# Attention on one Trainium2 core: two shifts of 128 bytes in the on-chip buffers

## The reference

```python
q = concat([q_C, rope(c_Q @ W_QR.T)]);  k = concat([k_C, rope(xn @ W_KR.T)])
weights = softmax(where(causal, clip(q @ k.T, -80, 80), -inf) / sqrt(192))
s = (weights @ v).reshape(B, S, H * D_H) @ W_O.T
g = silu(xn @ weight + lora(xn, router))
return x + s * g
```

## The kernel before

| buffers | begins at, before | remainder by 256 | after the change |
|---|---|---|---|
| cos, sin, qr_h/l, wo_first, rows_h0/l0, scale0 | 16,512 and on | 128 | 0 |
| absorb_h/l, cq_h/l, merged_h | 43,136 and on | 128 | 0 |
| causal | 77,952 | 128 | 0 |
| ones (128 bytes) | 78,976 | 128 | 128 |
| x_all and all of prepare's own (turn_h/l at 0, xt_h/l and b_h/l at 128) | 79,104 and on | as before | as before |
| key_slot 0 to 2, value_slot 0 and 1 | 79,104 and on | 0 | 0 |
| set 1: q_h1, q_l1, rot_hh1, rot_l01; rows_h1/l1 | 87,296 and on | 0 | 0 |
| prob, prob_h, prob_l, total1 | 120,064 to 152,832 | 0 | 0 |
| total0, rows0 | 178,048 | 128 | 0 |
| set 0: rot_l00, rot_hh0, q_l0, q_h0; merged_l | 186,240 and on | 128 | 0 |
| sums, head_rows | 219,008 and on | 128 | 0 |

## Time and profile before

### The profile page before, as it was taken

The page is one execution under the profiler, slowest core; times in us unless marked ns, Lnnn a source line. Parts: engine busy times, 40 slices in busy tenths (PEclk is TensorE's granted clock), DMA queues, the critical chain, the costliest instruction groups (busy, mean ns, idle before and its releaser), DMA issues.

```text
span 1417.7 us, 27675 instructions
## 1 busy us (share of the span) xinstructions
PE 1381.3 (97%) x9810; PEld 1156.7 (82%) x9810; DVE 1144.5 (81%) x1339; ACT 781.9 (55%) x861; POOL 125.7 (9%) x175
## 2 busy tenths in 40 slices
PE   7999689999999999999999999999999999999998
PEld 6888568778788888888888889888899688878887
DVE  7666378898898898989889898898788888967664
ACT  4232357666666666666666666666656656533221
POOL 0000111201101101010010100111100011012221
PEclk9999899999999999999999999999999999999999
DMA  7332664545435333334242432444412233166552
GB/s 291 118 100 79 193 199 150 173 138 150 122 96 149 107 108 85 120 87 126 63 122 85 104 110 63 118 153 140 134 56 61 69 109 115 49 197 173 174 159 89
DMA packets 110769, 174.91 MB, mean 123 GB/s; under 512 B 9608, under 2 KB 65160, under 8 KB 108168
## 3 DMA queue, kind: packets, MB, share of 16 engines
q1 hardware_dynamic: 93880, 108.99, 24.6%
q0 software_dynamic: 16016, 63.80, 15.4%
q10 hardware_dynamic: 832, 1.57, 0.5%
HBM read 125.83 MB, written 48.50 MB: 123 GB/s over the span
## 4 chain that ended last, share of the span: by engine, by line
PE 72%; DVE 9%; ACT 3%; DMA 2%; issue 2%; POOL 0%; SPq 0%; DVEq 0%; ACTq 0%; POOLq 0%
PE score_ps L1244 29%; PE out_ps L1266 19%; PE score_ps L1363 3%; PE score_ps L1365 3%; PE score_ps L1364 3%; DVE prob_l L1560 3%; ACT prob_h L1423 2%; DVE prob L1547 1%; DVE prod L1519 1%; PE out_ps L1285 1%; PE out_ps L1289 1%; PE out_ps L1286 1%; DVE total L1555 1%; PE score_ps L1214 1%; PE score_ps L1215 1%
## 5 line engine op out<-in xcount | busy, mean ns | idle before, releaser
L1423 ACT CAST prob_h<-prob 128x1024 fp32r<-128x1024 f32 (+1 forms) x288 | 289.6, 1006 | 237.3 <-DVE prob L1542 189.6
L1560 DVE TENSOR_TENSOR prob_l<-prob,prob_h 128x1024 fp32r<-128x1024 f32 (+1 forms) x288 | 336.0, 1167 | 39.6 <-ACT prob_h L1423 38.2
L1244 PE MATMUL score_ps<-q_h,key_slot 64*128 64x512 f32 x1792 | 365.8, 390 | 0.0
L1417 ACT ACTIVATE prob<-score_ps 128x1024 f32<-128x1024 f32 (+1 forms) x288 | 281.9, 979 | 145.8 <-PE score_ps L1244 96.5
L1266 PE MATMUL out_ps<-prob_h,value_slot 64*128 64x512 f32 (+1 forms) x1792 | 351.9, 378 | 0.7
L1555 DVE TENSOR_TENSOR total<-total,prob 128x1024 f32<-128x1024 f32 (+1 forms) x256 | 294.9, 1152 | 0.0
L1542 DVE TENSOR_SCALAR prob<-prob 128x1024 f32<-128x1024 f32 x224 | 155.1, 692 | 70.4 <-ACT prob L1417 70.1
L1266 PEld LDWEIGHTS out_ps<-prob_h,value_slot 64*128 64x128 f32 x1792 | 180.8, 184 | 35.5 <-DVE prob_l L1560 6.8
L1244 PEld LDWEIGHTS score_ps<-q_h,key_slot 64*128 64x128 f32 x1792 | 180.8, 184 | 28.1 <-issue 5.1
L1244 PE MATMUL score_ps<-rot_hh,key_slot 64*128 64x512 f32 x896 | 181.8, 388 | 0.0
L1244 PE MATMUL score_ps<-q_l,key_slot 64*128 64x512 f32 x896 | 181.6, 387 | 0.0
(11 more groups left out here) (210 smaller groups left out, 2005.2 us busy)
## 6 DMA issues: line engine op xcount, KB each, us to landing
key_slot<-keys SPq DMA_DIRECT2D x144, 256.0 KB, 2.6
value_slot<-values SPq DMA_DIRECT2D x144, 128.0 KB, 2.3
rot_hh<-turned POOLq DMA_DIRECT2D x30, 512.0 KB, 6.3
heads_rows<-head_rows POOLq DMA_DIRECT2D x15, 1024.0 KB, 9.7
turned<-rot_hl POOLq DMA_DIRECT2D x14, 1024.0 KB, 5.2
rows<-heads_rows SPq DMA_DIRECT2D x28, 512.0 KB, 5.7
rot_l<-turned POOLq DMA_DIRECT2D x30, 256.0 KB, 7.6
x_in<-in_x SPq DMA_DIRECT2D x16, 256.0 KB, 2.7
```

The costliest lines, as they stand in the source:

```text
L1244: mm = pe.matmul(score_ps[:, half, c * 512:(c + 1) * 512], keys_of[ROWS[r], :], moving[par][ROWS[r], half * HW + c * 512:half * HW + (c + ...
L1417: nc.scalar.activation(prob[half][:, 0:width], score_ps[:, half, 0:width], ACT.Exp, scale=QK_SCALE).then_inc(exp_done, 1)
L1423: nc.scalar.copy(prob_h[half][:, 0:width], prob[half][:, 0:width]).then_inc(high_done, 1)
L1560: nc.vector.tensor_tensor(p_l, p, p_h, ALU.subtract).then_inc(split, 1)
```

## The change

The unused `edge` on the right grows from 24 to 56 words of float32 (96 to 224 bytes), so all of `Top` moves down by 128 bytes. `ones` (128 bytes) is allocated ahead of the cosines instead of behind `causal`, so the buffers of `Persistent` other than `ones` move up by 128 bytes, and what lies behind it stays. No instruction, wait, transfer or size of an operand changes.

```diff
 WO_FIRST = 13
-EDGE = 24
+EDGE = 56
...
+        self.ones = sb("ones", [P, 32], F32)
         ((self.cos, self.sin, self.qr_h, self.qr_l), (self.wo_first,),
...
         self.causal = sb("causal", [P, CT], F32)
-        self.ones = sb("ones", [P, 32], F32)
```

## The result

The changed kernel takes 1410.43 us (median of 5 runs, 1409.48 to 1411.62) against 1418.6 for the kernel before (5 runs, 1416.91 to 1419.74). The ratio of the mean times is 0.9945, with a 95% interval from 0.9930 to 0.9959: 7.8 us less, and 8.2 by the medians, where 7.2 were forecast. With five runs the median of the kernel before is 1418.6, where the three runs known at the forecast gave 1417.05. The profiled execution took 1410.43 us, its span is 1408.9.

What follows compares the result with a forecast made beforehand. TensorE, busy 97% of the span, was taken to bound the kernel. Attention's 5.35 us plus projection's 1.87 made 7.2 us, taking the median from 1417.05 to 1409.8 us, with a range of 1406.0 to 1413.3.

Steps and rivals of the forecast that it cites:

- The third witness: Prepare: turn_h and turn_l at 0 against b_h and b_l at 128 take 233 ns a step, slow like odd tiles.
- (a): Attention: right-hand buffers go to 0 and agree with the keys, so even units match odd ones; 5.35 us gained.
- (b): Projection: left persistent buffers go to 0, odd tiles fall from 11.17 to 10.90; seven tiles gain 1.87 us.
- Tile 1's gain is given back: Projection: tile 1 brings nothing, as TensorE waits 0.8 us for VectorE's rows_l after tile 2 and that chain doesn't shorten.
- (c) to (e): Attention's VectorE work, 6.28 us a FULL pair, fits TensorE's 6.80; cq, absorb, qr, other buffers and short stretches gain nothing.
- (e): Short stretches after the latent run at 232 ns though 0 against 0; gain between 0 and 1.9 us, taken as 0.
- Nothing moves: Rival: the units' difference comes from place in SBUF or of the code, not the remainder; 1417.0 us, chance 0.08.
- Half of it: Rival: only projection gains, 1415.2 us, chance 0.05, or only attention gains, 1411.7 us, chance 0.05.
- Slower: Rival: the regular pace needs 128, so even tiles and 256-column steps lose and attention gains nothing; 1420.8 us, chance 0.03.
- More of it: Rival: attention's short stretches after the latent speed up too, 1.9 us more; 1407.9 us, chance 0.09.
- The rule in bold: TensorE is slow where weights and moving operand have different remainders by 256 bytes, 232.0 against 226.7 ns a step in attention.

Runs made afterwards that it cites:

- e7_prepare: Changed kernel with prepare's split weights as narrow and wide tensors, so wide rows, xt, b_h, b_l, turn_h, turn_l lie at 128; 1410.56 us, ratio 0.9941 to the kernel before.
- e8_again: The changed kernel run once more, nothing altered, as a yardstick; 1410.6 us, ratio 0.9943 to the kernel before.
- e3_all_128: Kernel before plus a 128-byte pad ahead of the key slots, putting all of attention and projection at remainder 128; 1411.84 us, ratio 0.9946.
- e1_edge: Kernel before with only the edge grown from 24 to 56 words, left persistent buffers staying at 128; 1413.47 us, ratio 0.9966.
- e2_ones: Kernel before with only ones moved in front, right-hand buffers staying where they were; 1418.83 us, ratio 1.0003.
- e9_order: Changed kernel with gaps: merged_l, rows_l0 and rows_h1 at 128, merged_h, rows_h0 and rows_l1 at 0; one execution, 1414.02 us.
- e4_keys_128: Changed kernel with the key and value slots alone at 128, the rest at 0; 1425.31 us, ratio 1.0048 to the kernel before.

## Why the prediction was right

**The basis.** The forecast took one set of operands as the state before and the other as the state after, and the trace of the changed kernel shows just that: 226.7 ns a step in unit 10 and couples that are equal to 0.02 us. The third witness, the products in prepare, was the check that it is a matter of two operands; e7_prepare brought those to one remainder, and they reached 227 ns.

**How near the number is, is partly luck.** The forecast of 1409.8 lies 0.6 us below the measured median because two misses offset each other: it started from 1417.05, 1.5 us below the later median of before, and its gain of 7.2 is 1.0 us short of the 8.2 by the medians (0.6 by the ratio). The gain is made up of the parts that follow.

**(a), attention, 5.35 us.** Measured from the start of unit 0 to that of unit 15: 1108.64 - 161.78 = 946.86 before, 1103.12 - 162.00 = 941.12 after, 5.74 less. Units 6, 8, 10 and 12 gave 0.48, 0.77, 1.08 and 1.32. Units 0 to 5 together gave 0.17, where 0.23 was put for unit 4; so small a term can't be tested, for unit 4 alone took 45.59 us in the changed kernel and 46.36 in e7_prepare with the same remainders. The mis-sized term is unit 14, put at 1.54 by carrying the series on. By stretch, before:

```profile
995.18:1108.64 113.46, 113.20 (x930) 107.45 (x928) 96.52 (x97) 70.86 (x72) 4.70 (x7) 1.00 0.28 81
```

and after:

```profile
991.55:1103.12 111.57, 111.30 (x931) 96.00 (x929) 96.40 (x97) 70.91 (x72) 4.20 (x7) 1.00 0.28 82
```

The difference is 1.89 us. Unit 14 makes no rotated queries for a next couple (`has_second` is false), which leaves VectorE less to do in its first pairs; by the starts in the trace its third FULL pair already ran at TensorE's own pace (6.93 us, and 6.80 after), while unit 12's took 7.20 and 7.14. So more of its pairs run at TensorE's own pace than two more pairs would add, and each of them gains. That the lighter load of VectorE is the cause is argued from the code. Carrying on a series of units was sound only while they had the same work.

**(b), projection, 1.87 us.** The odd tiles from 3 to 15 fell from about 11.16 to 10.88, seven times 0.28, as put. "Tile 1's gain is given back" failed. Tile 1 fell from 11.25 to 11.02, and the wait after tile 2, which cost the kernel before 1.0 us (tile 2 took 11.89 there and 10.88 after), was not there in the profiled execution, so the trace shows 3.3 us less from tile 0 to the end. By e8_again that wait differs by 0.4 us between two executions of one kernel; the step took one execution's wait for a fixed chain. The text of (b) also gives to the ones alone what needs both edits: merged_l moves with the edge.

**(c) to (e)** held. VectorE covers the faster pace: its three operations take 1219, 1226 and 695 ns in unit 10, and the view of TensorE's waits shows none for VectorE from unit 6 to 14, before or after. Nothing moved in the latent matmuls (120 ns a step), and the short stretches stayed at 232 ns, the bound of 0. That the jump from 128 to 0 had upset them is excluded by the changed kernel, where there is none. That a stretch takes some steps to fall into the regular pace fits the start of the changed kernel's unit 10, where after the first step four take 0.93 us (232 ns each) and the next five 1.13 (226).

**The rivals.** "Nothing moves" fell with the first trace, and its reasons (the half of SBUF, the code's place) with e3_all_128. The Trainium skill (SBUF — State Buffer, Who interferes with whom) calls TensorE's two read ports independent and says that it never waits on anyone; the same matmuls run at 226.7 or 232.0 ns a step here by an address alone, which speaks against taking it that addresses don't matter to TensorE. On "Half of it", e1_edge and e2_ones show that the edge alone gives attention's part, and that projection's part needs both edits. "Slower" fell too: the regular pace needs no 128, for the even tiles, moved from 128 to 0, went from 10.90 to 10.88. "More of it" fell with (e).

**What was only a reading** is that weight loads and moving reads get in each other's way. The rule in bold, weights against moving operand, is right for a stretch in which all matmuls agree or all stand apart, and too simple for a mixed one: there the agreeing steps are slow too. What the runs show is that the regular pace came only where all weights and moving operands of a stretch had one remainder. One form of the reading, that only the next weights must agree with the present moving operand, was tried in e9_order and fell; the mechanism stays open.

## What to carry to other kernels

Look whether a pair of buffers that serve the same instructions in turn run at the same pace; a difference of 2% between them is a comparison that costs no run. Where TensorE sets the pace with long runs of 512-column matmuls (in fp32r, each with weights of its own, as here; no other kind was tried), let all its operands, weights and moving, begin at one remainder by 256 bytes, and keep row pitches a multiple of 256 too, as e7_prepare did. The remainders 0 and 128 served alike. A buffer whose size is no multiple of 256 bytes, allocated ahead of them, is enough to break it. Both edits have to be made together where operands come from both ends of the memory.

## What was not expected

- The cost doesn't grow with the number of matmuls that stand apart: one in three cost 0.11, 0.21 or 0.32 us of 10.88 in an output tile, two in three 0.11 or 0.21, all three 0.11, 0.28, 0.31, 0.32 or 0.36.
- Differences of 32, 64, 96, 128 and 192 bytes cost nearly the same in attention, 87.0 to 87.4 us for unit 10 or 11 in place of 86.0, while in an output tile 192 bytes cost 0.11 us and 96 bytes 0.36.
- In stretches where only some steps agree (set 0's scores apart, values and probabilities in agreement) the agreeing steps are slow as well: a FULL pair of the kernel before took 6.94 us with 18 of its 30 steps apart, 6.97 with all of them (e4_keys_128), 6.80 with none.
